# Attention with rows' maxima subtracted by TensorE on scores that have keys on partitions, instead of flipped probabilities

## The reference, cut to what matters

```python
h = _layernorm(x) * (1 + ca) + sa
Q = einsum('bsh,hd->bsd', h, Wq) + bq ; K = Q ; V = Q
scores = einsum('bqh,bkh->bqk', Q, K) / sqrt(128)
x = x + ga * einsum('bqk,bkh->bqh', softmax(scores, -1), V)
h = _layernorm(x) * (1 + cb) + sb
route = sigmoid(h @ Wr + br) ; e = argmax(route)       # 8 experts
x = x + gb * (gelu(h @ W1[e]) @ W2[e]) * max(route)
```

## Time and profile before

| | |
|---|---|
| median of 3 runs | 344.84 us (344.6 to 344.9) |
| the profiled execution | 345.61 us, its span 343.9 us |
| granted TensorE clock | 0.998 of full over the span |
| PE busy | 327.3 us, 95% |
| PE weight loads | 300.9 us, 88% |
| DVE busy | 280.1 us, 81% |
| ACT busy | 217.6 us, 63% |
| POOL busy | 192.6 us, 56% |
| loads of an x tile | 256 KB each, 3.0 us to land |

### The profile page before, as it was taken

One profiled execution on the slowest core, in us unless ns is written; L12 is line 12 of the kernel. 1 busy time (PEld: TensorE's weight loads), 2 busy tenths in 40 slices (PEclk: granted clock), 3 DMA queues, 4 the chain that ended last, 5 costly groups with the idle time before them and its releaser, 6 DMA issues. The chain is left out here.

```text
span 343.9 us, 8445 instructions
## 1 busy us (share of the span) xinstructions
PE 327.3 (95%) x2582; PEld 300.9 (88%) x2582; DVE 280.1 (81%) x1135; ACT 217.6 (63%) x472; POOL 192.6 (56%) x224
## 2 busy tenths in 40 slices
PE   4999999999999999999999899999999999999992
PEld 3687788889889888988887789899999999999992
DVE  4578898898898889888997886899897777778662
ACT  2588987887798779878867564544444444444440
POOL 4017457545744664475456146777756537765655
PEclk9999999999999999999999999999999999999999
DMA  3383124557567558841544722566689744553500
GB/s 116 97 282 114 32 70 116 122 114 106 145 114 92 129 149 141 297 141 58 151 116 134 273 86 92 141 198 198 205 255 311 245 135 144 133 156 103 168 22 20
DMA packets 34349, 49.21 MB, mean 143 GB/s; under 512 B 4304, under 2 KB 25971, under 8 KB 34304
## 3 DMA queue, kind: packets, MB, share of 16 engines
q1 hardware_dynamic: 27328, 31.66, 38.5%
q0 software_dynamic: 6368, 16.92, 12.9%
q10 hardware_dynamic: 608, 0.08, 0.1%
HBM read 28.15 MB, written 20.96 MB: 143 GB/s over the span
## 5 line engine op out<-in xcount | busy, mean ns | idle before, releaser
L1472 POOL DMA_INDIRECT sorted_rows<-payload,slots x64 | 63.9, 998 | 81.1 <-DVE slots L1108 66.2
L1499 POOL DMA_INDIRECT out_dram<-y_out,tokens x71 | 75.6, 1065 | 39.8 <-issue 22.6
L649 PE MATMUL mixed<-down_slot,hidden 128*128 128x128 f32 x568 | 70.2, 276 | 0.6 <-ACT hidden L845 0.6
L549 PE MATMUL mixed<-v_sb,probs_t 128*128 128x128 f32 x512 | 69.0, 278 | 0.0
L649 PEld LDWEIGHTS mixed<-down_slot,hidden 128*128 128x128 f32 x568 | 66.6, 192 | 1.1 <-ACT hidden L845 1.1
L788 ACT ACTIVATE probs<-scores,row_max 128x512 f32<-128x512 f32 x64 | 44.1, 689 | 35.9 <-DVE row_max L999 34.6
L549 PEld LDWEIGHTS mixed<-v_sb,probs_t 128*128 128x128 f32 x512 | 62.2, 192 | 0.2
L999 DVE TENSOR_REDUCE row_max<-scores 128x1 f32<-128x512 f32 x64 | 44.1, 689 | 19.5 <-PE scores L526 19.4
L830 ACT ACTIVATE f_hi<-side 128x256 fp32r<-128x256 f32 (+1 forms) x39 | 14.2, 365 | 42.8 <-PE side L611 41.4
L536 PE MATMUL flipped<-ident,probs 128*128 128x128 f32 x256 | 39.5, 277 | 0.4 <-ACT probs L788 0.3
L796 ACT ACTIVATE probs_t<-flipped 128x512 f32<-128x512 f32 x64 | 37.8, 593 | 0.0
(11 more groups left out here) (209 smaller groups left out, 771.5 us busy)
## 6 DMA issues: line engine op xcount, KB each, us to landing
rows<-sorted_rows SPq DMA_DIRECT2D x32, 388.0 KB, 3.7
x_tile<-in_L_attn_inputs_dram SPq DMA_DIRECT2D x16, 256.0 KB, 3.0
payload<-stored_gates SPq DMA_DIRECT2D x16, 256.0 KB, 9.3
sorted_rows<-pad_rows SPq DMA_DIRECT2D x9, 388.0 KB, 4.8
w_parts<-in_L_ffn_W_dram SPq DMA_DIRECT2D x1, 2048.0 KB, 10.9
rows<-sorted_rows SPq DMA_DIRECT2D x7, 194.0 KB, 2.4
out_dram<-y_out,tokens POOLq DMA_INDIRECT x71
sorted_rows<-payload,slots POOLq DMA_INDIRECT x64
```

The lines of the kernel that those rows point to most:

```text
L549: last = nc.tensor.matmul(mixed[j % 2][:, 0:H], probs_t[:, j % 2, k * P:(k + 1) * P], v_sb[:, b.p, k, :], start=(k == 0), stop=(k == J - 1))
L649: last = nc.tensor.matmul(mixed[t % 2][:, u * H:(u + 1) * H], hidden[:, t % 2, f, u * P:(u + 1) * P], down_slot[:, t % 3, f, :], start=(f ...
L1472: nc.gpsimd.indirect_dma_start(rows_dram, bass.IndirectOffsetOnAxis(ap=slots[:, c:c + 1], axis=0), payload[:, b.q, j, :], None).then_inc(s ...
L1499: nc.gpsimd.indirect_dma_start(out_rows, bass.IndirectOffsetOnAxis(ap=tokens[:, t % RING, u:u + 1], axis=0), y_out[:, t % RING, u, :], Non ...
```

## The change

Because the scores are symmetric, the block with keys j on partitions and all queries in its columns is the same matmul as before. A query's maximum now belongs to a column. ScalarE scales the identity by the negated maxima (`make_shift`), TensorE multiplies a matrix of ones with that and adds it to the four score banks (`subtract_max`), and the exponents come out as `probs_t` at once. `flip_probs`, `copy_probs` and the accumulated `den` are gone; the sum comes from a column of ones behind the values, so that a mix has 129 columns. All four score banks (`scores`, `flipped`) now hold one batch, both `mixed` banks hold two row blocks each. The second normalisation of tiles 2 and 3 moves from VectorE to ScalarE, which needs `offset2` from GpSimd. The slots are written anew: slot k has the mixes of batch k and the scores and exponents of batch k+1, projects batch k+2 and normalises batch k+3; there are 15 of them, between a prologue and a longer ending. `invert2` now follows the scatter in GpSimd's queue. The weights' splits go to slots 1 to 4, two experts each.

```diff
-            for k in range(-2, B):
+            for k in range(B - 1):
...
-        W1_SPLITS = {k: range(k * E // 2, (k + 1) * E // 2) for k in range(2)}
+        W1_SPLITS = {k: range(2 * (k - 1), 2 * k) for k in range(1, E // 2 + 1)}
+
+        banks = (*scores, *flipped)
+
+        def mix_bank(j):
+            return mixed[j // 2][:, (j % 2) * 2 * P:(j % 2) * 2 * P + H + 1]
...
-                wait(pe, exp_done, J * b.n + j - 1)
+                wait(pe, exp_done, J * (b.n - 1) + j + 1)
                 mine = slice(j * P, (j + 1) * P)
-                o = scores[j % 2][:]
+                o = banks[j][:]
...
+            def subtract_max(b):
...
+                pe.wait_ge(shift_made, J * (b.n + 1))
+                for j in range(J):
+                    nc.tensor.matmul(banks[j][:], ones_r[:], shift[:], start=False, stop=True,
+                                     skip_group_check=True).then_inc(shifted, 1)
+
+            def mix(b, j):
...
+                if j == 0:
+                    pe.wait_ge(exp_done, J * (b.n + 1))
+                    pe.wait_ge(v_ready, b.n + 1)
...
+                wait(pe, x1_ready, J * (b.n - 1) + 2 * (j // 2) + 2)
                 for k in range(J):
...
+                    last = nc.tensor.matmul(mix_bank(j), probs_t[:, k, j * P:(j + 1) * P], v_sb[:, b.p, k, :],
+                                            start=(k == 0), stop=(k == J - 1))
...
+                before2, before, now, after, after2, after3 = (batch_at(k + d) for d in range(-2, 4))
                 mix(now, 0)
...
+                score(after, 0)
+                if k == 0:
+                    flip_xn(after2)
+                else:
+                    project(after2)
                 mix(now, 1)
-                score(after, 0)
-                flip_probs(now, 3)
+                score(after, 1)
+                if k == 0:
+                    project(after2)
                 places(before2)
...
                 mix(now, 2)
-                flip_xn(after2)
+                score(after, 2)
+                score(after, 3)
                 flip_xn2(before)
+                mix(now, 3)
+                subtract_max(after)
+                flip_v(after2)
+                router(before)
+                flip_xn(after3)
+                flip_h2(before)
...
+            mix(last_one, 0)
+            flip_rows(0)
+            mix(last_one, 1)
+            places(batch_at(B - 3))
+            mix(last_one, 2)
+            flip_xn2(last_but_one)
+            up(0)
             mix(last_one, 3)
+            flip_rows(1)
             router(last_but_one)
             down(0)
...
+            def make_shift(b, j):
...
+                act.wait_ge(max_found, J * b.n + j + 1)
+                if j == 0:
+                    wait(act, shifted, J * b.n)
+                c = b.p * J + j
+                nc.scalar.activation(shift[:, j * P:(j + 1) * P], ident[:], ACT.Identity, scale=row_max[:, c:c + 1]
+                                     ).then_inc(shift_made, 1)
+
             def exps(b, j):
                 if not real(b):
                     return
...
+                act.wait_ge(shifted, J * b.n + j + 1)
+                wait(act, attn_done, J * b.n)
+                nc.scalar.activation(probs_t[:, j, :], banks[j][:], ACT.Exp).then_inc(exp_done, 1)
...
+                if k > 0:
+                    input_t(after2)
                 for e in W1_SPLITS.get(k, ()):
                     split_w1_hi(e)
+                logit_exp(before2)
+                ffn_input(before2)
+                normalize2(before)
+                make_shift(after, 0)
+                if k == 0:
+                    input_t(after2)
+                else:
+                    query(after2)
+                normalize1(after3, (0, 1))
+                make_shift(after, 1)
+                if k == 0:
+                    query(after2)
+                normalize1(after3, (2, 3))
+                make_shift(after, 2)
+                make_shift(after, 3)
+                router_input(before)
+                for j in range(J):
+                    exps(after, j)
...
-                dve.wait_ge(exp_done, J * b.n + 2 * pair + 2)
+                dve.wait_ge(attn_done, J * b.n + 2 * pair + 2)
                 c = b.p * J + 2 * pair
-                nc.vector.reciprocal(den_inv[:, c:c + 2], den[:, c:c + 2]).then_inc(den_ready, 1)
+                nc.vector.reciprocal(den_inv[:, c:c + 2], mixed[pair][:].rearrange("p (u c) -> p u c", u=2)[:, :, H]
+                                     ).then_inc(den_ready, 1)
...
+                    nc.vector.tensor_scalar_mul(neg_mean2[:, b.p, :], moments2[:, b.p, :, 0], -1.0)
```

VectorE's slot in the new order (added lines only; the old slot stands in the kernel above):

```diff
+                ln1(after3)
+                variance1(after3)
                 if planning:
                     early_plan(0)
...
+                choose(before2, 0)
+                find_max(after, 0)
+                choose(before2, 1)
+                normalize2(before, (0,))
+                choose(before2, 2)
+                normalize2(before, (1,))
+                choose(before2, 3)
+                choose(before2, 4)
+                invert_den(now, 0)
+                choose(before2, 5)
+                residual(now, 0)
+                residual(now, 1)
+                find_max(after, 1)
+                choose_slots(before2, 0)
+                ln2_stats_of(now, 0)
+                choose_slots(before2, 1)
+                ln2_stats_of(now, 1)
+                choose_slots(before2, 2)
+                find_max(after, 2)
+                find_max(after, 3)
+                split_q(after2)
                 if planning:
                     early_plan(1)
...
+                ln2_moments_of(now, 1)
+                invert_den(now, 1)
+                residual(now, 2)
+                residual(now, 3)
+                ln2_stats_of(now, 2)
+                ln2_stats_of(now, 3)
+                values(after2)
+                ln2_moments_of(now, 2)
+                add_bias(before)
+                ln2_moments_of(now, 3)
```

GpSimd's slot:

```diff
             def slot(k):
-                before2, before, after2 = batch_at(k - 2), batch_at(k - 1), batch_at(k + 2)
-                invert1(after2)
-                invert2(before)
-                token_ids(before2)
+                before2, now, after3 = batch_at(k - 2), batch_at(k), batch_at(k + 3)
+                invert1(after3)
                 for e in W1_SPLITS.get(k, ()):
                     split_w1_lo(e)
+                token_ids(before2)
                 scatter(before2)
+                invert2(now)
```

More of the change, by code:

```diff
@@ L1222, in slot @@
             def slot(k):
-                before2, before, now, after, after2 = (batch_at(k + d) for d in range(-2, 3))
+                before2, before, now, after, after2, after3 = (batch_at(k + d) for d in range(-2, 4))
                 planning = k == EARLY_AFTER + 3
-                ending = k == B - 1
-                find_max(now, 1)
-                residual(before, 2)
-                ln2_stats_of(before, 2)
-                if k >= 0:
-                    ln1(after2)
-                ln2_moments_of(before, 2)
@@ L1269, in slot @@
-                if ending:
-                    split_lo(1)
-                normalize2(before, (0, 1))
-                find_max(after, 0)
-                normalize2(before, (2, 3))
-                choose_slots(before2, 0)
-                residual(now, 1)
-                invert_den(now, 1)
-                ln2_stats_of(now, 1)
-                ln2_moments_of(now, 1)
-                choose_slots(before2, 1)
-                choose_slots(before2, 2)
+            first, second = batch_at(0), batch_at(1)
@@ L1283, in _ @@
+            values(first)
+            find_max(first, 0)
+            find_max(first, 1)
+            ln1(batch_at(2))
+            variance1(batch_at(2))
+            find_max(first, 2)
+            find_max(first, 3)
+            split_q(second)
+            values(second)
             attention_slots(slot)
@@ L1373, in _ @@
             last_but_one, last_one = batch_at(B - 2), batch_at(B - 1)
[L1374 removed]
+            before_these = batch_at(B - 3)
+            for part in range(3):
+                choose(before_these, part)
+            normalize2(last_but_one, (0,))
+            choose(before_these, 3)
+            normalize2(last_but_one, (1,))
+            choose(before_these, 4)
+            choose(before_these, 5)
+            dve.wait_ge(early_ready, 1)
+            dve.wait_ge(w1_split, E)
+            dve.wait_ge(w2_loaded, 16)
+            fill_slots(0)
+            split_lo(0)
+            invert_den(last_one, 0)
+            choose_slots(before_these, 0)
+            residual(last_one, 0)
+            choose_slots(before_these, 1)
+            residual(last_one, 1)
+            choose_slots(before_these, 2)
+            for j in (0, 1):
+                ln2_stats_of(last_one, j)
+            invert_den(last_one, 1)
+            for j in (0, 1):
+                ln2_moments_of(last_one, j)
             for j in (2, 3):
```

(4 more changed lines are left out.)

189 lines of the change are left out of this document (80 added, 109 removed).

## The result

The changed kernel takes **350.97 us** (350.14 to 351.48, four runs) beside 344.87 for the kernel before (344.6 to 345.11, four runs): a ratio of 1.0175, interval 1.0153 to 1.0196. It is slower by 6.1 us, where 338.9, 5.9 faster, was forecast. The profiled execution took 350.14 for a span of 348.1. Ratios compare the faster executions of two kernels; the profiled executions of experiment two and of the first run with both edits in experiment five were slow ones, so from these two only slots and waits are read.

What follows compares the result with a forecast made beforehand. TensorE, filling each 11.77 us slot, was the bound. Slots of 11.27, a prologue 4.2 later and 2.4 for splits put the second up projection 5.9 earlier: 344.84 - 5.9 = 338.9 us; range from 333 less half a microsecond to 344.5.

Steps and rivals of the forecast that it cites:

- prologue: Scores, maxima, shifts, subtraction, exponents and query ahead of the first mix: it starts at 24.3 us, 4.2 later than before.
- slot 0: First mix of batch 0 to that of batch 1: 10.6 us, with nothing older to serve.
- slots 1 to 4: Slots holding the moved weights' splits: 11.0 us for the first, 11.27 for each other, plus 2.4 for splits.
- slots 5 to 12: Steady attention slots without splits: 11.27 us each.
- slot 13: Slot with a piece of the early plan between split and bias: 12.1 us.
- slot 14: Last slot, no batch 16 to project but the plan's last piece: 10.6 us.
- down(0): First down projection of the experts, after the last attention mixes: near 202.6 us, against 208.89 before.
- The tiles of the experts: Experts' work from 230 us on, which fills TensorE: as long as before, nothing given back.
- The walk: One steady slot followed instruction by instruction: 11.27 us with 0.28 of waiting, 0.50 saved against 11.77.
- the rows show a third of that: GpSimd's eight weights' splits stretch VectorE by 3.3 us, not their whole length, which would give near 345.
- The rival: GpSimd's power behind four scatters delays normalisation, deciding once a scatter takes over 1.7 us: 349 us, chance 0.10.
- the splits' own bounds: Cost of the moved weights' splits, taken as 2.4 us: from nothing to a full split twice in each slot.

Runs made afterwards that it cites:

- experiment two: Kernel after with GpSimd's subtractions of the weights' splits moved to slots 5 to 8, ScalarE's copies left in slots 1 to 4: 1.0182 of the kernel before.
- both edits: Kernel after with all splits in slots 0 and 1 and no drain ahead of batch 11's scatters: 0.9894 and 0.9863 on slower chips, 0.9951 on the quiet one.
- experiment five: Kernel after without batch 11's drain: 1.0113; also with early splits: 0.9894, again 0.9863; drain kept, power ahead of scatters in slot 13: 1.0079, with early splits 1.0008.
- experiment seven: Kernel after on a quiet chip: splits in slots 0 and 1 0.9964 (343.5 us), no drain for batch 11 1.0147 (350.49), both 0.9951 (343.11).

## Why the prediction was wrong

Against the forecast (profiled execution, first mix of batch 15 at 204.03 for 195.0) the terms are: prologue -0.2, slot 0 +0.7, slots 1 to 4 +4.5 (51.75 against 44.8 and 2.4), slots 5 to 12 +0.5, slot 13 -0.3, slot 14 +3.8; then +1.3 to down(0). The tiles of the experts are as long as forecast (135.2 for 135.4). That is 10.1 in span, and the median of the runs lies 0.8 above the profiled one, where it was taken 0.8 below; with 0.3 more around the span that makes the 12.1 us between 338.9 and 350.97.

**The walk was right.** A slot of 11.27 was 11.33, the first mix at 24.3 came at 24.07, four subtractions of 0.96 took 1.05, and a mix of 129 columns costs what one of 128 did; shifts took 0.40, not 0.29, with no harm. With both causes taken away the first mix of batch 15 is at 195.19 for a forecast of 195.0, by luck in part, for slot 0 ran at the lower clock and no split was left in slots 2 to 4.

**Step that failed, one: the splits, "the rows show a third of that".** The earlier trace rows had a multiply at 1.14 for 0.17 and a split of q at 1.72 for 0.68; I added the extra of four rows, got 3.3 of eight splits' 10 us, and took that fraction as the price. That was how often the old order happened to meet the hold, not its price. VectorE's timeline of the kernel before under the first four subtractions, then GpSimd's:

```profile
28.05 0.85 DVE L906 BATCH_NORM_STATS2 stats<-x_tile 128x6 f32<-128x128 f32 x4
...
30.35 0.68 DVE L999 TENSOR_REDUCE row_max<-scores 128x1 f32<-128x512 f32 x1
30.95 0.33 DVE L1018 SCALAR_TENSOR_TENSOR payload<-mixed,den_inv,x_tile 128x128 f32<-128x128 f32 x1
```

```profile
27.82 5.00 POOL L1478 TENSOR_TENSOR w_parts<-w_parts 128x512 fp32r<-128x512 f32 x4 [7.33 <-ACT w_parts L823]
```

Under the first and the third subtraction stood statistics, a maximum and a residual, which take their usual time. Under the second and fourth stood one small multiply each, the 1.14 and 0.98 of the earlier trace rows, held to the subtraction's end. The four rows are thus four held instructions of eight subtractions, less what of each subtraction was already over. In the new slots both subtractions meet held kinds, the normalisation and the comparison. By the Trainium skill (SBUF — State Buffer, section "two separate sides") GpSimd and a VectorE instruction with two SBUF inputs or in a two-port mode share one pair of ports, and whichever starts first has it for its whole instruction. By that rule the sum was near 345 in the prediction, and the traces agree with it: 1.36 and 1.27 under subtractions of 1.25, and 0.85, 0.68 and 0.33, as always, for the statistics, the maximum and the residual above, which have one input in SBUF or none. Of two holds, 2.5 us, TensorE waits 1.6 to 1.9 in each of slots 2 to 4 and the slots are 1.7 to 2.1 longer; in slot 1, where no mask is due, 0.8 (11.87 against 11.08 to 11.11 with one subtraction there or none). I gave 0.8 for two, less 0.2. The slots cost 7.0 us over a walk without splits (51.75 against 44.8), where 2.4 was forecast. The rows to ask for were VectorE's between the normalisation and the mask, and what TensorE does when the mask is late.

**Step that failed, two: "slot 14 10.6" and GpSimd's queue.** The rival named the mechanism, the power behind the scatters, but let it decide by a scatter's price, 1.7, which stayed at 1.27, now and then 1.6 (174.05 to 175.67). It was decided by a drain that the code shows ahead of two batches' scatters and the sum left out. Before, the power went first, and the first scatter of batch 11 started at 182.82, at its row numbers (6.14 idle, ended by them), so no row showed the drain. With it out of the way slot 14 is 10.60 to 10.62, as forecast, 0.61 of waiting for the mask included; of the 3.8 too much, 2.25 is more waiting (2.86) and the rest, 1.5, matmuls at the lower clock behind it. Yet in run time the drain is worth less, 0.4 us with early splits and an estimated 1.0 to 2.4 with late ones, for part of what comes earlier there waits for the next drain (experiment seven).

**Smaller:** slot 0 has 0.88 of waiting for batch 2's values, left out (+0.7). Ahead of down(0) the flip of batch 14 waits 1.27 for VectorE's batch_count, behind the filling of slots; I had half a microsecond (+1.3). The range ended at 344.5, under the upper end of the splits' own bounds, a full hold twice in each slot.

## What to carry to other kernels

When work of GpSimd is moved, list what VectorE does at the new place. Here small multiplies, normalisations, the comparison and the split of q were held to the end of GpSimd's subtraction; statistics, maxima and residuals were not. Price each held one at the subtraction's full length, less a wait that VectorE had there, and don't spread the stretched rows of the old place over all subtractions. When an operation moves behind another in a queue, list everything that stands ahead of it, drains and waits for another engine's half too: one that shows no row may be hidden by a wait that the change removes. And try the moved work on the engine that would be held: here 0.69 us of VectorE inside its own wait replaced 1.25 of GpSimd that held it, and came out as good as the splits at the start.

## What the hardware showed that I had not expected

- With a drain between them, the last scatter of one batch and the first of the next start 6.7 to 13.2 us apart, by the slot (11.6 in the kernel after, 176.93 to 188.49). Begun 14 us behind the last scatter's start, a drain still took 4.6 us.
- The same kernel before takes 344 to 345 us on two chips and 363 to 368 on three. TensorE's long pauses there begin after some 200 us.
- Beside one and the same run of subtractions on GpSimd, VectorE's small multiply took 1.14 for 0.17, while its statistics, maximum and residual took no longer than elsewhere (0.85 for four, 0.68, 0.33).
- A wait of 1.9 us was followed by matmuls of 0.63 for 0.40 in one execution (granted clock 0.81 in the window 70 to 76.7) and not in another, at the same place of the same schedule: 1.4 us more for one slot.
